# Three parts and seven products in the first conditional network of a two-layer AdaLN feed-forward kernel

## What is computed

```python
def _L0_cond_ref(...):            # F = 1376, RANK = 16, SCALE = 0.5
    gate = lora_add(einsum('bnh,fh->bnf', x, W_gate), x, A_gate, B_gate)
    up = lora_add(einsum('bnh,fh->bnf', x, W_up), x, A_up, B_up)
    act = jax.nn.silu(gate) * up
    return lora_add(einsum('bnf,hf->bnh', act, W_down), act, A_down, B_down)
x = x + _L0_ffn_ref(_L0_cond_ref(x, ...), ...)      # ffn0: weights times low-rank scales, 1792 wide
x = x + _L1_ffn_ref(_L1_cond_ref(x, ...), ...)      # cond1: one linear with adapters; ffn1: int4 weights
```

## Time and profile before

| | |
|---|---|
| median of 3 runs | 620.11 us (620.07 to 622.11) |
| span of the profiled execution | 618.3 us |
| TensorE busy | 611.3 us, 99% |
| VectorE busy | 444.9 us, 72% |
| ScalarE busy | 313.2 us, 51% |
| GpSimd busy | 243.6 us, 39% |
| cond, from the start to its last gate/up tile | 0 to 179.9 us |
| cond down b | 179.9 to 209.8 us |

### The profile page before, as it was taken

The page is one execution under the profiler, slowest core; times in us unless marked ns, Lnnn a source line. Parts: engine busy times, 40 slices in busy tenths (PEclk is TensorE's granted clock), DMA queues, the critical chain, the costliest instruction groups (busy, mean ns, idle before and its releaser), DMA issues.

```text
span 618.3 us, 8106 instructions
## 1 busy us (share of the span) xinstructions
PE 611.3 (99%) x2958; PEld 499.8 (81%) x2958; DVE 444.9 (72%) x544; ACT 313.2 (51%) x415; POOL 243.6 (39%) x194
## 2 busy tenths in 40 slices
PE   8999999999999999999999999999999999999997
PEld 6787888788778878788878888888788888888885
DVE  4585564644458999886247887645879998999987
ACT  5675615344354444452014444334657886478860
POOL 3670010000000006861034566530004889958896
PEclk9999999999999999999999999999999999999999
DMA  8750022101013111411211101152222121222203
GB/s 257 192 147 28 25 88 89 52 18 46 21 49 94 35 34 56 151 60 60 68 35 68 55 15 57 42 108 69 82 73 99 64 72 52 103 68 80 74 1 137
DMA packets 24826, 45.19 MB, mean 73 GB/s; under 512 B 10132, under 2 KB 12404, under 8 KB 24724
## 3 DMA queue, kind: packets, MB, share of 16 engines
q1 hardware_dynamic: 22484, 40.97, 21.3%
q0 software_dynamic: 2016, 3.19, 1.9%
q10 hardware_dynamic: 288, 0.52, 0.2%
HBM read 40.74 MB, written 2.10 MB: 69 GB/s over the span
## 4 chain that ended last, share of the span: by engine, by line
PE 98%; DMA 1%; SPq 0%; DVE 0%; ACT 0%; issue 0%
PE ps_down L2010 8%; PE ps_down L2011 7%; PE ps_down L2012 7%; PE ps_up L2010 4%; PE ps_up L2011 4%; PE ps_up L2012 4%; PE ps_gate L2142 3%; PE ps_gate L2199 3%; PE ps_gate L2198 3%; PE ps_up L2198 3%; PE ps_gate L2143 3%; PE ps_gate L2144 3%; PE ps_gate L2010 3%; PE ps_up L2199 3%; PE ps_m L2198 3%; PE ps_m L2199 3%
## 5 line engine op out<-in xcount | busy, mean ns | idle before, releaser
L876 POOL TENSOR_TENSOR act_lo<-up,act_hi 128x512 fp32r<-128x512 f32 x14 | 18.1, 1294 | 174.0 <-ACT act_hi L1176 174.0
L2010 PE MATMUL ps_down<-act_hi,w_hi 128*128 128x512 f32 x176 | 69.0, 392 | 0.0
L2011 PE MATMUL ps_down<-act_lo,w_hi 128*128 128x512 f32 x176 | 68.6, 390 | 0.0
L2012 PE MATMUL ps_down<-act_hi,w_lo 128*128 128x512 f32 x176 | 68.5, 389 | 0.0
L917 POOL TENSOR_TENSOR up_sum<-up_sum,up_more 128x1024 f32<-128x1024 f32 x14 | 33.7, 2406 | 61.9 <-DVE up_more L1551 61.9
L1416 DVE TENSOR_TENSOR w_lo<-w_raw,w_hi 128x512 fp32r<-128x512 f32 (+3 forms) x41 | 39.2, 955 | 13.3 <-ACT w_hi L990 9.3
L990 ACT ACTIVATE w_hi<-w_raw 128x1024 fp32r<-128x1024 f32 (+3 forms) x30 | 26.5, 884 | 43.6 <-PE ps_down L2012 17.9
L2012 PEld LDWEIGHTS ps_down<-act_hi,w_lo 128*128 128x128 f32 x176 | 33.0, 188 | 7.0
L1551 DVE SCALAR_TENSOR_TENSOR gate_sum<-ps_up,s_group,gate_sum 128x1024 f32<-128x1024 f32 x28 | 35.8, 1280 | 3.8 <-PE ps_up L2199 3.7
L2010 PEld LDWEIGHTS ps_down<-act_hi,w_hi 128*128 128x128 f32 x176 | 33.1, 188 | 6.6
L2011 PEld LDWEIGHTS ps_down<-act_lo,w_hi 128*128 128x128 f32 x176 | 33.1, 188 | 6.5
(11 more groups left out here) (321 smaller groups left out, 1799.5 us busy)
## 6 DMA issues: line engine op xcount, KB each, us to landing
w_int<-in_ffn_gu SPq DMA_DIRECT2D x14, 512.0 KB, 3.5
w_raw<-in_cond_gu SPq DMA_DIRECT2D x9, 512.0 KB, 5.0
w_raw<-in_ffn_gu SPq DMA_DIRECT2D x9, 512.0 KB, 3.5
w_raw<-in_ffn_dn SPq DMA_DIRECT2D x8, 448.0 KB, 3.2
w_int<-in_ffn_dn SPq DMA_DIRECT2D x8, 448.0 KB, 3.2
xp<-in_x SPq DMA_DIRECT2D x8, 256.0 KB, 5.3
w_raw_third<-in_ffn_gu SPq DMA_DIRECT2D x4, 512.0 KB, 3.5
xp<-in_x SPq DMA_DIRECT2D x1, 2048.0 KB, 9.9
```

Source lines behind the costliest of these rows:

```text
L2010: nc.tensor.matmul(ps[0:m, :], w_hi[0:r, s, cols], rhs_hi(k, r), start=start and n == 0, stop=False)
L2011: nc.tensor.matmul(ps[0:m, :], w_hi[0:r, s, cols], rhs_lo(k, r), start=False, stop=False)
L2012: last = nc.tensor.matmul(ps[0:m, :], w_lo[0:r, s, cols], rhs_hi(k, r), start=False, stop=stop and n == len(ks) - 1)
```

## The change

The first conditional network goes from two parts of 6 and 5 tiles to three of 4, 3 and 4. Its tiles 2 to 10 use seven products; tiles 0 and 1 stay plain. The weights of a seven-product tile are combined by three GpSimd sums (`cond_sums`), and the x operands once, at the start. The first two weight pieces of the next tile are rounded by ScalarE before the former tile's activations. There is a third down phase ("cond down c"), which takes the place of "cond down b" with tail and adapters. Adapter factors are kept in a ring of 1024 columns and loaded in five loads (`B_LOADS`), the first two as before by both queues and by GpSimd, the last three by SyncE; all tiles use the copy of rows. GpSimd orders a_dn, loads four of it instead of six, does act_lo of the conditional tiles except the last of parts a and b, the block sums of ffn0's first tile and five of ffn0's nine x sums.

```diff
+COND_TILES, COND_FIRST = (4, 3, 4), (0, 4, 7)
+COND_STEPS = ("2", "3", "1", "4", "5", "g0", "6", "7", "u1")
+COND_SLOT = {2: 1, 3: 0, 4: 0, 5: 1, 6: 0, 7: 1, 8: 0, 9: 1, 10: 0}
+T_ROUNDS = {2: (0, 1), 6: (4, 5), 8: (6, 7), 10: (8, 9)}
+B_LOADS = ((0, 4), (4, 7), (7, 9), (9, 11), (11, 13))
-A_DN_POOL = 6
+A_DN_POOL = 4
 # SyncE
+            load(down_b, 0)
+            copy_b(6)
+            load(down_b, 1)
+            sp.wait_ge(cond_seven, cond_step(6, "u1"))
+            for b in range(NB):
+                load_b(sp, b, 2, b_again_in[1])
+            load(down_b, 2)
+            load(down_b, 3)
+            load(gu_c, 0)
+            copy_b(7)
+            load(gu_c, 1)
+            sp.wait_ge(down_ready, down_b.d0 + CH * HK)
+            for b in range(NB):
+                load_b(sp, b, 3, b_again_in[2])
+            load(gu_c, 2)
+            copy_b(8)
+            load(gu_c, 3)
+            copy_b(9)
+            sp.wait_ge(cond_seven, cond_step(8, "u1"))
+            for b in range(NB):
+                load_b(sp, b, 4, b_again_in[3])
+            load(down_c, 0)
 # ScalarE
+            def cond_tile(t):
+                cond_m2_to_sbuf(t)
...
+                if not last_of_part(t):
+                    for piece in range(2):
+                        cond_piece(t + 1, piece)
+                else:
+                    tile_hi(down_phase(t), 0, 0)
+                if t > 2 and not first_of_part(t):
+                    cond_act_hi(t - 1)
+                if t == 3:
+                    hi_of_pack()
+                cond_silu_gate0(t)
+                if not last_of_part(t):
+                    cond_piece(t + 1, 2)
+                    cond_silu_gate1(t)
+                    hi_of_b(t + 1)
+                    return
+                if t == NKD - 1:
+                    for p in range(NKD, NBP):
+                        hi_of_b(p)
+                cond_silu_gate1(t)
+                cond_act_hi(t)
+            def cond_down(ph):
+                t = COND_FIRST[ph.part + 1]
+                tile_hi(ph, 0, 1)
+                tile_hi(ph, 1, 0)
+                hi_of_b(t)
+                cond_piece(t, 0)
+                tile_hi(ph, 1, 1)
+                for piece in (1, 2):
+                    cond_piece(t, piece)
 # VectorE, cond_tile(t), waits left out
+                elif not first_of_part(t):
+                    cond_products(t - 1)
+                nc.vector.tensor_tensor(d, bank_b, m2, ALU.subtract).then_inc(cond_diff, 1)
+                    cond_piece(t + 1, 0)
+                nc.vector.tensor_tensor(e, bank_a, d, ALU.add).then_inc(cond_part, 1)
+                    cond_piece(t + 1, 1)
+                nc.vector.tensor_tensor(e, e, bank_c, ALU.add).then_inc(cond_both, 1)
+                nc.vector.tensor_tensor(e, e, bank_b, ALU.subtract).then_inc(cond_rest, 1)
+                if t == NKD - 1:
+                    for p in range(NKD, NBP):
+                        lo_of_b(p)
+                nc.vector.tensor_tensor(gate[0:m, :], bank_a, d, ALU.add).then_inc(cond_gate1, 1)
+                    cond_piece(t + 1, 2)
+                nc.vector.tensor_tensor(up[0:m, :], bank_c, e, ALU.add).then_inc(cond_up0, 1)
+                if inside and t > 2:
+                    lo_of_b(t + 1)
 # TensorE
+            def cond_tile(t):
+                pe.wait_ge(cond_piece_ready, 2 * count)
+                product(2, bank_c).then_inc(cond_seven, 1)
+                product(3, bank_b).then_inc(cond_seven, 1)
+                product(1, bank_a).then_inc(cond_seven, 1)
+                pe.wait_ge(cond_m2_copied, count)
+                product(4, bank_c, more=True).then_inc(cond_seven, 1)
+                for tile in T_ROUNDS.get(t, ()):
+                    t_down(tile)
+                pe.wait_ge(w_ready, cond_index(t))
+                pe.wait_ge(cond_diff, count)
+                product(5, bank_b, more=True).then_inc(cond_seven, 1)
+                pe.wait_ge(cond_both, count)
+                gate_up_adapters(bank_c, t, 0, 0).then_inc(cond_seven, 1)
+                pe.wait_ge(cond_part, count)
+                product(6, bank_a, more=True)
+                gate_up_adapters(bank_a, t, 0, 1).then_inc(cond_seven, 1)
+                pe.wait_ge(cond_gate0, count)
+                product(7, bank_c)
+                gate_up_adapters(bank_c, t, 1, 0).then_inc(cond_seven, 1)
+                pe.wait_ge(cond_rest, count)
+                gate_up_adapters(bank_b, t, 1, 1).then_inc(cond_seven, 1)
```

More of the change, by code:

```diff
@@ L835, in _ @@
                 pool.wait_ge(mask_ready, n + 1)
+            pool.wait_ge(ids_in[0], 16)
+            for b in range(BC):
+                load_a_gu(pool, b)
+            for b in range(BC):
+                load_b(pool, b, 0, b_in[b // BC])
+            pool.wait_ge(start_lo, len(start))
+            for n in (6, 7):
+                first, second = (x_block(half, c) for half, c in x_terms[n])
+                nc.gpsimd.tensor_tensor(cond_x_total[n][:, :, :], first, second, ALU.add).then_inc(cond_x_more, 1)
@@ L1009, in hi_of_b @@
                     return
[L1010 to L1015 removed]
+                if p > 0:
+                    act.wait_ge(b_ready, p)
@@ L2365, in _ @@
                 tile_steps(pe, ph, step, in_loop=False)
-                if ph.name == "cond down a":
-                    for j in range(3, CUT):
-                        t_down(phases[0], j)
             for g in groups:
```

935 lines of the change are left out of this document (586 added, 349 removed).

## The result

| | before | after |
|---|---|---|
| median | 620.25 us (620.07 to 622.11) | 638.27 us (637.96 to 639.89) |
| ratio | | 1.029 (95% interval 1.027 to 1.031) |
| span of the profiled execution | 618.3 us | 638.2 us |

The account below looks back on a forecast made before the run. TensorE, busy 99% of the span, was taken as the bound. The terms -12.2 + 0.4 + 0.7 + 5.9 + 4.0 = -1.2 gave span 617.1, with 1.8 outside it 618.9 us; range 613.5 to 624.0.

Parts of the forecast that it names:

- (c): Nine tiles and ffn0: VectorE's two-operand operations wait half a GpSimd instruction, 0.65, instead of 0.26 more; 627.5 us, chance 0.14.
- What is removed: Conditional tiles 2 to 10: 54 gate/up matmuls fewer, -12.2 us, all on the path.
- Down b: Down b: eight adapter loads on SyncE hold back column 2, wait 5.0, then 0.8 at column 3; +5.9 us.
- Before tile 2: Start and down a: extra a_dn pairs, x sums and roundings are covered; all at nothing, 1 us if one cover is short.
- The nine tiles: Tiles 2 to 10: VectorE operations longer beside GpSimd, waits of 0 to 0.3 in five tiles; +0.7 us, bounds 0 and 5.
- The last part: Last conditional down part and ffn0's first tiles: VectorE is the limit and TensorE waits; +4.0 us, bounds 2 and 6.
- (a): Last part: costs 1 us instead of 4, since five sums leave VectorE; 615.9 us, chance 0.15.
- (b): Down b: reload hidden, loads take 0.33 each on SyncE, 0.5 left of 5.9; 613.5 us, chance 0.09.
- (d): Tiles 8 to 10: loads behind SyncE's index reads come 1 us late each as well; 622 us, chance 0.10.

Follow-up runs that it names:

- e4: Changed kernel with GpSimd's two x sums at the start cut from 1024 columns to 64 each (computes something else, only its time is of use); 635.18 us.
- e7: Changed kernel with the start's two x sums, a_dn copy and two x roundings on VectorE behind the adapter factors, GpSimd's tile 3 weight sums earlier; 642.01 us.
- e11: Changed kernel, start reordered: products of tiles 0 and 1 ahead of four x roundings and one x sum, the other x sum on GpSimd; 637.43 us.
- e6: Changed kernel with ScalarE rounding the next tile's first two weight pieces behind the former tile's activations again, in tiles 3 to 10; 642.95 us.
- e5: Changed kernel with the next tile's adapter factors rounded half a tile earlier on ScalarE and VectorE, in tiles 4, 5, 7, 8 and 9; 637.61 us.
- e1: Changed kernel with down b's eight adapter loads moved from SyncE to GpSimd and column 3 rounded ahead of tile 7's adapter factors; 635.45 us.
- e13: e12 with SyncE loading tile 8's weights ahead of copying tile 7's adapter rows, and x roundings 3 and 1 made earlier; 625.29 us.
- e14: Kernel before with two TensorE waits put into its first down part, both 2.6 us; 629.45 us.
- e8: Changed kernel, last part reordered: tail adapter pieces and column 1 rounding earlier; tile 10's act_lo, block sums and x sums back on VectorE; 633.70 us.
- e10: e8 and two moves more: block column 2 and its tail rounded earlier, product 2's bank copied behind two x roundings instead of five; 631.36 us.
- e12: Changed kernel with e1 (tile 7's factors now behind weight pieces and evictions), e5, e10 and e11 combined; 626.53 us.
- e15: e12 with three moves: SyncE's loads of tile 8's and 9's weights and down a's first column earlier, GpSimd's a_dn loads earlier; 624.18 us.
- e9: Changed kernel with e1 (tile 7's factors now behind weight pieces and evictions), e5, e7 and e8 combined; 632.13 us.

## Why the prediction was wrong, by its own steps

I said 618.9, between 613.5 and 624.0, and gave slower 0.17. It was 638.3, and the slowest of my rivals, (c), was 627.5.

**What is removed** was right. Tile 4, which waits for nothing, lasts 10.51 (91.48 to 101.99), forecast 10.5; before, 11.9. Nine times the difference is 12.7, forecast 12.2.

**Down b** was right in its mechanism and size: eight loads over 8.0 instead of 8.7 us, one wait of 4.1 instead of 5.0 behind VectorE's cond_dn_lo. The second, forecast at 0.8, would have been 2 and is hidden by the 11 matmuls at 0.43 behind the first, which are not in my sum. Down b lasts 7.0 more than its 72 matmuls take at 0.2267, for a forecast of 5.9.

**"Before tile 2 ... all at nothing; 1 us if one cover is short"** is the step that failed most, +7.9. I had looked at the idle time of each engine for itself, and VectorE's time was enough for three x sums, 3.5. What I did not ask is when the pieces behind them would run: plain_lo at 22.98 instead of 18.6, and behind it in a row masked t, the t_rows, the adapter factors, SyncE's copies. The two x sums on GpSimd lie right beside, and e4 shows that they alone make 2.7 of it; the sum priced them at nothing for VectorE. With the x work behind the adapter factors (e7, e11) tile 2 began at 36.8 to 37.3, so most of the 7.9 hung on VectorE's queue; the price came back in part as waits of 4.6 and 1.9 in tile 2.

**The nine tiles**, +0.7 with bounds 0 and 5: 4.1, inside the bounds and not where I put it. Tiles 5 and 9 last 11.6 instead of the 10.5 of tile 4, and tiles 2 and 3 are some 1.0 longer each, without what t_down and half clock take. e was done at 7.7 in tile 5, not at 6.4. VectorE left tile 4 at 2.45 instead of 1.9, the first product took 1.05 from start to start instead of 0.61, the second piece 1.10. I had added 0.26 for each such operation, the mean of the earlier trace rows; it was 0.4 to 0.5. A mean over a long stretch counts all the operations that met no one; where GpSimd works back to back, as it does in these tiles, each one meets it. And I left out that t_down covers the delay in three of the tiles. With the 3.4 that this is over its forecast, the 1.1 of down b, 0.5 at half clock at the start of tile 2, and 0.8 in down a, where column 3 waited 0.5 for cond_dn_lo and which I had put at nothing, the 5.8 between forecast and measured of this stage are told.

**The last part**, +4.0: the third tile came at T + 57.3 instead of T + 48.6. At the product of 213.65 it was already 3.4 late (T + 19.3, forecast T + 15.9): the last product of tile 10 was as forecast (T + 3.5 for 3.3), but then ScalarE's 1.1 and the pairs beside GpSimd. From there it took 37.9 instead of 32.7. I had credited 3.6 for five x sums that leave VectorE and 1.2 against it; measured, moving all sums back saves 3.5 (T + 53.8), and 1.8 to 2.0 against the runs that have this part as in after and less half clock in it. The sign of this step was wrong. Some 1.4 of the 5.2 are half clock, as the next paragraph has it.

**The clock** stands nowhere in my prediction. The earlier trace rows show full clock throughout, and I took it for a constant, although the kernel before has none of the waits that I was forecasting. In the profiled execution of after the matmuls of the four stretches took about 8 us more (1.2, 2.2, 1.6, 2.7), but less of it reached the span. The 1.2 at the start may have in full. The 2.2 in down b took the place of column 3's wait. The 1.6 behind T did hardly: in e6, which runs at full clock there, product 4 of ffn0's first tile comes at T + 35.6 instead of T + 35.9, since VectorE and ScalarE set it. Of the last stretch 1.4 did: from product 4's wait to the third tile it is 21.4 with 13 matmuls at half clock, and 20.0 in e5, which has none, and in e1 and e4, which have 8. So at most some 3 us of the 19.9 are the clock's, an estimate from these rows. It is also the likely reason why the executions of after differ: the granted clock on record is 0.981 in the profiled one and 0.986 to 0.987 in the three that are 1.6 to 1.9 us shorter.

**Rival (c)** had the right mechanism, 0.65 or more for each VectorE operation beside GpSimd, and I put it where there was the least of it. I had the rule of the Trainium skill in hand (SBUF — State Buffer, section "Who interferes with whom"), that the two shut each other out for a whole instruction, and set it aside for a mean. This trace bears the rule out: 3.41 for 1.23, beside a GpSimd sum of 3.0.

**Rivals (a) and (b)** did not come: the last part lies 12.7 over TensorE's own T + 44.6, not the 1 of (a), and the eight loads took 7.96, not the 3 of (b). Its 0.33 for one load does not stand in the earlier trace rows but in SyncE's single rows, and is the DMA without the index read.

**Rival (d)** was right as well and hidden: in e13, otherwise faster, it costs 2.0 in tile 8.

## What to carry to other kernels

Do not price an operation beside GpSimd by the mean over a long stretch where both engines have work without a gap; take the rows at which they meet, and remember that the delay hits the queue behind it. Where TensorE is the limit, allow for half clock behind a wait of a few microseconds even where the kernel before runs at full clock throughout: in e14 it makes a wait of 2.6 cost 4.4. Where another engine is late anyway, the half clock only fills the wait that would have come. And cover is not only the idle time of an engine but its place in that engine's queue: from e8 to e10 and from e12 to e15 only places were changed, for 2.3 us each, and moving tile 7's adapter factors back (e9, e12) made the load behind their copy late.
